# Issuing the first three row loads of the first state tile directly behind the store of those rows

## The chip, the cores and the metric

The kernel runs on one core of one Trainium2 chip. The metric is the device time of one launch in microseconds (us); lower is better. The number compared is the median of several launches.

## The reference

The input x is 4 x 1024 tokens of 128 features. Three blocks change it in turn, each with a residual: a mixture-of-experts layer at half weight, a state-space (Mamba) layer, and the same experts again at half weight.

```
x = x + 0.5 * ffn(layernorm(x))
x = x + mamba(layernorm(x))
x = x + 0.5 * ffn(layernorm(x))

ffn:   cw = softmax(x @ w_router) * softmax(x @ w_gating / 0.1), divided by its sum
       out = sum over 8 experts e of cw[e] * ((silu(x @ w_gate[e]) * (x @ w_up[e])) @ w_down[e])
mamba: xs, z = split(x @ W_in);  xc = silu(causal_conv4(xs) + conv_b)
       dt0, B, C = split(xc @ W_x);  dt = softplus(dt0 @ W_dt + b_dt)
       for each token: h = exp(dt * A) * h + (dt * xc) * B;  y = sum over 16 states of h * C
       out = ((y + xc * D) * silu(z)) @ W_out
```

## The kernel before, in words

**Tiles.** The 4096 tokens are cut into eight tiles of 512 tokens. Each tile goes through the experts twice (kind 0 before the Mamba layer, kind 1 behind it), which makes 16 positions. `ORDER` (line 36) fixes their order: tiles 0 to 3 of kind 0, then kinds 1 and 0 by turns. A position has 32 slots: 8 experts times 4 chunks of 128 hidden features. Slot 50, say, is in position 1. A slot is three passes of TensorE for the gate (`first_g`, line 713), a SiLU on ScalarE (`silu`, line 1024), three passes for the up projection (`first`, line 724), their product on VectorE (`first`, line 851) and a down matmul (`down`, line 734), which follows two slots later. Gates run two slots ahead of the up projections. There are three PSUM banks for gates, so the gate of slot i waits for the SiLU of slot i-3 (line 711), and two for up projections, so the up projection of slot i waits for the product of slot i-2 (line 722). At the end of each expert `acc` (line 841) multiplies the expert's output with its token weights, which `cw_load` (line 658) has broadcast from DRAM, and GpSimd issues a DMA that adds it to `ACC` (line 1127).

**The Mamba layer beside it.** Its work on a tile is woven into the slots. `before(t)` (line 181) makes the projections, the convolution, `b_x` (B, C and the input of dt) and dt. `bc_store` (line 643) writes the 32 rows of B and C of 512 tokens from SBUF to the DRAM tensor `BCD`. `scans(t)` (line 267) then goes through the 16 states. For state m (counted over all tiles) `bc_load` (line 650) broadcasts one row of B and one of C to all 128 partitions, into one of `BR` = 3 buffers of `BCB`; `s_b` (line 932) multiplies B with dt * xc; `s_da` (line 1090) makes the decays of two states on ScalarE; `s_scan` (line 943, twice) is the recurrence; `s_hc` (line 951) multiplies with C; and GpSimd issues two DMAs that add the result to `Y` (line 1139).

**What sets the order.** `timetable()` (line 53) runs once on the host. It plays generators (`before`, `scans`, `prep`, `tail`, `closing`) against estimated clocks and appends their steps to one list, `steps`. Each engine then issues its own steps in the order of that list, and waits in order, on semaphores. SyncE's steps, the loads and stores, cost nothing on these clocks. So a step of SyncE takes the place in SyncE's queue at which its generator emitted it.

**Around the change.** For tile 0 the list holds, with the steps of SyncE in bold: `b_x`, **`bc_store` 0**, product 45, `b_dtl`, down 43, `acc` 10, **`cw_load` 13**, gate 48, the `b_dt` steps, ..., `b_dx`, down 47, `acc` 11, **`cw_load` 14**, gate 52, `b_y`, product 50, down 48, gate 53, **`bc_load` 0, 1, 2**, `s_b` 0, `s_b` 1, product 51, `s_da` 0, down 49, the first scan of state 0, gate 54, product 52, down 50, gate 55, product 53, down 51, `acc` 12, **`cw_load` 15**, gate 56, product 54, the layer norm `ln_sum` 3, the second scan, `s_hc` 0, **`bc_load` 3**, and so on. `cw_load` g waits for the `acc` three before it (line 657), so `cw_load` 13 waits for `acc` 10 and `cw_load` 14 for `acc` 11. `bc_load` 0 waits for the landing of `bc_store` 0 (line 647); the loads 0 to 2 wait for nothing else.

The loads are emitted by this helper (line 261), which in the kernel before is called in `scans` alone, at its start and after each `s_hc`:

```
def bc_loads(upto):
    while loaded[0] < upto and loaded[0] // NS in stored:
        step("bc_load", loaded[0])
        loaded[0] += 1
```

Of the kernel before, what the change touches and what calls it, by code (L numbers as in the profile page):

```python
# [31 lines left out]
BR = 3  # L32
# [20 lines left out]
def timetable():  # L53
# [8 lines left out]
    def step(*what, after=0.0, **work):  # L62

        steps.append(what)
        for e, c in work.items():
            clock[e] = max(clock[e], after) + c
            after = clock[e] + SIGNAL[e]
        return after

    def give(b, sem, value, at):  # L70
        free.append((at, b, (sem, value)))
        free.sort(key=lambda f: f[0])

    def until(at):
        while clock["pe"] < at:
            yield False

    def until_v(at):
        while max(clock["v"], clock["pe"]) < at:
            yield False  # L80

    def take():
        while not free or free[0][0] > clock["pe"]:
            yield False
        return free.pop(0)[1:]
# [7 lines left out]
    def rows_of_x():  # L93

        while xn["lock"] or clock["pe"] < xn["at"]:
            yield False
        xn["lock"] = True

    def norm(b, what):
        while ln["lock"]:  # L100
            yield False
        ln["lock"] = True
        q = norms[0]
        norms[0] += 1
        yield from rows_of_x()
        yield from calm()
        at = step("ln_sum", q, b, xn["by"], what, after=clock["pe"], a=1.6)
        yield True
        yield from calm()
        at = step("ln_square", q, b, after=at, a=1.6, p=2.0)  # L110
        yield from until(at + .3)
        at = step("ln_x", q, b, after=at, a=1.5)
        ln["lock"] = False
        yield from until(at + 0.7)
        bk = yield from take()
        at = step("ln_t", q, bk, pe=.6)
        xn.update(by=("m_tr", q + 1), lock=False)
        return q, bk[0], at
# [62 lines left out]
    def before(t):  # L181

        haste.add("before")
        q, b, at = yield from norm(t % XR, ("x1", t))
        haste.clear()
        at = step("b_xn", t, q, b, after=at, a=.52)
        yield from until_v(at + LATEST)
        at = step("b_xl", t, q, b, after=at, v=.75)
        give(b, "v_rm", t + 1, at)
        yield from until(at)  # L190
        for j in range(2):
            bk = yield from take()
            win_at = step("b_in", t, j, bk, pe=.69, a=1.04)
            give(bk[0], "a_win", 4 * t + j + 1, win_at)
            yield True
        yield from until_v(win_at)
        step("b_halo", t, v=.2)
        for q in range(3):
            for j in range(2):
                at = step("b_conv", t, q, j, v=.67)  # L200
                if q != 1:
                    yield True
            if q < 2:
                bk = yield from take()
                give(bk[0], "a_win", 4 * t + q + 3, step("b_in", t, q + 2, bk, pe=.69, a=.52))
                yield True
        yield from until(at - .5)
        for j in range(2):
            at = step("b_silu", t, j, after=at, a=.62)
        yield True  # L210
        yield from until(at)
        yield from rows_of_x()
        bk = yield from take()
        at = step("b_x", t, bk, xn["by"], pe=1.75, a=.9)
        step("bc_store", t)
        xn.update(by=("c_bcd", 16 * (t + 1)), lock=False, at=at + 2.0)
        stored.add(t)
        yield from until_v(at + LATEST)
        at = step("b_dtl", t, bk[0], after=at, v=.61)
        give(bk[0], "v_bc", t + 1, at)  # L220
        yield from until(at)
        for j in range(2):
            bk = yield from take()
            at = step("b_dt", t, j, bk, pe=.47, a=1.1)
            give(bk[0], "a_relu", 2 * t + j + 1, at)
            yield True
        yield from calm()
        at = step("b_soft", t, after=at, a=4.5)
        yield True
        yield from until_v(at + LATEST)  # L230
        at = step("b_dx", t, after=at, v=2.4)
        dt_at[t] = at - 1.2
        decays()
        ready[t] = at
        yield from until_v(at)
        yield from calm()
        step("b_y", t, after=at, a=1.1)
        begun_y.add(t)
        yield True
# [7 lines left out]
    def decays(must=False):  # L247

        m = decayed[0]
        if m < NT * NS and m // NS in dt_at and m + BURST <= done[0] + NA and (must or (  # L250
                dt_at[m // NS] < clock["pe"] + .5 and clock["a"] < clock["pe"] + CALM)):
            at = step("s_da", m, after=dt_at[m // NS], a=2.56 + 1.24 * BURST)
            for k in range(BURST):
                decay_at[m + k] = at
            decayed[0] = m + BURST

    def calm():
        while clock["a"] > clock["pe"] + CALM:
            yield False
# [6 lines that stand above are left out]
# [71 lines left out]
    def mamba_streams():  # L337
        t = begun["closing"]
        if "closing" not in streams and t < NT and t in scanned:
            streams["closing"] = closing(t)  # L340
            begun["closing"] += 1
        t = begun["scans"]
        if "scans" not in streams and t < NT and t in ready and ready[t] < clock["pe"]:
            streams["scans"] = scans(t)
            begun["scans"] += 1
        t = begun["before"]
        if "before" not in streams and t < NT and t in x1 and t <= begun["scans"] and t - 2 in put:
            streams["before"] = before(t)
            begun["before"] += 1
# [42 lines left out]
    for i in range(total):  # L392
# [30 lines left out]
        if p + 1 < NPOS and r >= (PREP if p != 1 else LATER) and p + 1 not in prepared:  # L423
            kind, t = ORDER[p + 1]
# [742 lines left out]
```

## Time and profile before

| what | value |
|---|---|
| median of 3 runs | 1301.04 us (1297.74 to 1301.64) |
| the profiled execution's own time | 1303.95 us |
| its span, first to last instruction | 1302.2 us |
| granted TensorE clock, mean over the span | 0.991 |
| TensorE busy | 1259.6 us (97%) |
| VectorE busy | 1121.7 us (86%) |
| ScalarE busy | 925.3 us (71%) |
| GpSimd busy | 366.8 us (28%) |
| DMA | 208.55 MB, mean 160 GB/s |

The profile describes one execution. Engines are PE (TensorE matmul), PEld (its weight loads), DVE (VectorE), ACT (ScalarE), POOL (GpSimd) and SP (SyncE); a small q marks an engine's instruction queue. Busy time of PE is modelled, since matmuls are pipelined. Times on timelines are microseconds from the start of the span.

### The profile page before, as it was taken

What the parts mean: (1) busy time and instruction counts of PE and PEld (TensorE: products, weight loads), DVE (VectorE), ACT (ScalarE), POOL (GpSimd) and SP (SyncE); (2) the same over time, 40 slices, a digit from 0 to 9 for tenths busy, and PEclk for the clock granted to TensorE, in tenths of its full rate; (3) what the DMA queues carried; (4) which work ended last, traced back from release to release, by engine and by line L of the source; (5) the groups of instructions that cost most, each with busy time, mean ns of one, the idle gap of its engine ahead of it and who ended that gap; (6) DMA issues with size and microseconds to landing.
All of it is one profiled execution on the core that took longest, in us unless ns stands there. A gap on an engine that the chain in (4) does not pass through costs nothing.

```text
span 1302.2 us, 15232 instructions
## 1 busy us (share of the span) xinstructions
PE 1259.6 (97%) x4608; PEld 841.3 (65%) x4608; DVE 1121.7 (86%) x1468; ACT 925.3 (71%) x1757; POOL 366.8 (28%) x438
## 2 busy tenths in 40 slices
PE   5999799999999999999999999999999999999998
PEld 4666566666666666666666666666666665666665
DVE  3554599999999999999989999999999998998343
ACT  6545688878797878887948878698866887653421
POOL 0100134324232322433323332342323323332000
PEclk9999899999999999999999999999999999999899
DMA  6521488789788988987888978987888786895221
GB/s 204 134 54 33 100 177 197 160 176 196 161 181 184 181 173 188 208 177 169 183 180 188 194 171 178 181 191 170 188 175 186 174 186 149 186 197 119 50 64 41
DMA packets 125809, 208.55 MB, mean 160 GB/s; under 512 B 15008, under 2 KB 27808, under 8 KB 125728
## 3 DMA queue, kind: packets, MB, share of 16 engines
q0 software_dynamic: 52128, 94.92, 40.8%
q1 hardware_dynamic: 73600, 112.68, 32.8%
q8 instruction: 36, 0.59, 0.2%
q14 instruction: 45, 0.37, 0.1%
HBM read 109.77 MB, written 2.88 MB: 87 GB/s over the span
## 4 chain that ended last, share of the span: by engine, by line
PE 65%; DMA 12%; ACT 9%; DVE 8%; issue 5%; POOL 2%; SPq 0%; DVEq 0%; ACTq 0%; POOLq 0%
PE PS L734 23%; PE PS L679 13%; PE PS L681 13%; PE PS L680 13%; DMA Y<-HS 7%; DMA ACC<-YE 3%; DVE HS L943 2%; DVE HB L851 2%; DVE HS L951 2%; ACT DA L1090 1%; ACT HB L1024 1%; DMA BCB<-BCD 1%; ACT L1024 1%; PE PS L755 1%; ACT L1090 1%
## 5 line engine op out<-in xcount | busy, mean ns | idle before, releaser
L734 PE MATMUL PS<-HB,WD 128*128 128x512 f32 x1024 | 525.3, 594 | 0.0
L1024 ACT ACTIVATE HB<-PS 128x512 f32<-128x512 f32 x512 | 293.1, 596 | 279.8 <-PE PS L681 277.4
L851 DVE TENSOR_TENSOR HB<-PS,HB 128x512 f32<-128x512 f32 x512 | 347.2, 679 | 113.9 <-PE PS L681 71.7
L679 PE MATMUL PS<-XH,WG 128*128 128x512 f32 x512 | 386.6, 755 | 6.1 <-DVE XH L906 2.0
L1139 POOL DMA_DIRECT2D Y<-HS x252 | 219.7, 949 | 511.0 <-DVE HS L951 319.5
L734 PEld LDWEIGHTS PS<-HB,WD 128*128 128x128 f32 x1024 | 191.8, 189 | 44.3 <-issue 3.4
L679 PE MATMUL PS<-XH,WU 128*128 128x512 f32 x512 | 209.5, 409 | 10.1 <-DVE HB L851 9.8
L1127 POOL DMA_DIRECT2D ACC<-YE x110 | 104.1, 947 | 369.3 <-DVE YE L841 339.4
L681 PE MATMUL PS<-XH,WG 128*128 128x512 f32 x512 | 203.2, 397 | 0.0
L681 PE MATMUL PS<-XH,WU 128*128 128x512 f32 x512 | 202.0, 395 | 0.0
L680 PE MATMUL PS<-XH,WU 128*128 128x512 f32 x512 | 201.0, 393 | 0.0
L680 PE MATMUL PS<-XH,WG 128*128 128x512 f32 x512 | 200.5, 392 | 0.0
L679 PEld LDWEIGHTS PS<-XH,WG 128*128 128x128 f32 x512 | 97.3, 190 | 120.8 <-issue 67.3
L680 PEld LDWEIGHTS PS<-XH,WG 128*128 128x128 f32 x512 | 97.9, 191 | 110.1 <-issue 108.4
L1090 ACT ACTIVATE DA<-XS,aneg 128x512 f32<-128x512 f32 x256 | 164.4, 713 | 2.6 <-DVE HS L943 1.7
L932 DVE TENSOR_TENSOR HS<-BCB,DX 128x1026 f32<-128x1026 f32 (+1 forms) x128 | 155.7, 1220 | 9.2 <-DMA BCB<-BCD 9.2
L943 DVE TENSOR_TENSOR_SCAN HS<-DA,car,HS 128x512 f32<-128x512 f32 x128 | 161.8, 1274 | 0.0
L951 DVE TENSOR_TENSOR HS<-BCB,HS 128x1024 f32<-128x1024 f32 x128 | 156.0, 1219 | 1.1
L943 DVE TENSOR_TENSOR_SCAN HS<-DA,HS 128x513 f32<-128x513 f32 x128 | 155.0, 1219 | 0.1
L679 PEld LDWEIGHTS PS<-XH,WU 128*128 128x128 f32 x512 | 96.7, 189 | 37.0 <-DVE HB L851 15.9
L1024 ACT ACT_TABLE_LOAD x86 | 110.3, 1283 | 2.8 <-PE PS L681 1.1
L681 PEld LDWEIGHTS PS<-XH,WU 128*128 128x128 f32 x512 | 96.7, 189 | 23.2
(104 smaller groups left out, 1127.3 us busy)
## 6 DMA issues: line engine op xcount, KB each, us to landing
BCB<-BCD SPq DMA_DIRECT2D x128, 512.0 KB, 5.6
Y<-HS POOLq DMA_DIRECT2D x252, 256.0 KB, 6.7
CWB<-CWD SPq DMA_DIRECT2D x128, 256.0 KB, 4.3
ACC<-YE POOLq DMA_DIRECT2D x110, 256.0 KB, 5.3
XT<-in_L_attn_x_dram SPq DMA_DIRECT2D x8, 256.0 KB, 5.9
WD<-in_L_ffn_w_down_dram SPq DMA_DIRECT2D x8, 256.0 KB, 6.1
out_dram<-XT SPq DMA_DIRECT2D x8, 256.0 KB, 3.1
HS<-in_L_ffn_w_gate_dram SPq DMA_DIRECT2D x6, 256.0 KB, 5.0
```

The source lines that it names most:

```text
L679: pe.matmul(o, w[0], m[0], start=first, stop=False)
L680: pe.matmul(o, w[0], m[1], start=False, stop=False)
L681: z = pe.matmul(o, w[1], m[0], start=False, stop=last)
L734: pe.matmul(expert(g), WD[:, e, c, :], HB[:, i % NH, :], start=c == 0, stop=c == FC - 1).then_inc(S["m_dn"], 1)
L851: v.tensor_tensor(H, up(i), H, ALU.mult).then_inc(S["v_h"], 1)
L932: v.tensor_tensor(HS[:, m % HR, :, 0:w], rows.unsqueeze(1).broadcast_to([P, 2, w]), DX[:, t % 2, :, 0:w], ALU.mult).then_inc(S["v_db"], 1)
L943: v.tensor_tensor_scan(H, DA[:, m % NA, j, 0:w], H, car[:, j, n:n + 1] if t % 2 else 0.0, ALU.mult, ALU.add).then_inc(S["v_sc"], 1)
L951: v.tensor_tensor(H, BCB[:, m % BR, 1, :].unsqueeze(1).broadcast_to([P, 2, T]), H, ALU.mult).then_inc(S["v_hc"], 1)
L1024: a.activation(HB[:, i % NH, :], gate(i), ACT.Silu).then_inc(S["a_sil"], 1)
L1090: z = a.activation(DA[:, m % NA, j, 0:T], XS[:, t % 2, j, 3:3 + T], ACT.Exp, scale=aneg[:, j, n:n + 1])
L1127: gp.dma_start(ACC[:, :], YE[:, n % 2, :], accum_op=ALU.add).then_inc(S["c_acc"], 16)
L1139: gp.dma_start(Y[:, t % 2, j, :], HS[:, m % HR, j, 0:T], accum_op=ALU.add).then_inc(S[f"c_y{j}"], 16)
```

## The change

Directly behind the store of tile 0's rows, and for tile 0 only, the helper is called with `BR` = 3, so that `bc_load` 0, 1 and 2 stand right behind `bc_store` 0 in SyncE's queue and ahead of `cw_load` 13 and 14. The call at the start of `scans(0)` then finds nothing left to emit. All other steps keep their order.

```
--- before.py
+++ after.py
@@ -215,6 +215,8 @@
         step("bc_store", t)
         xn.update(by=("c_bcd", 16 * (t + 1)), lock=False, at=at + 2.0)
         stored.add(t)
+        if t == 0:
+            bc_loads(BR)
         yield from until_v(at + LATEST)
         at = step("b_dtl", t, bk[0], after=at, v=.61)
         give(bk[0], "v_bc", t + 1, at)
```

## Rows read from the trace of the kernel before

**Rows 1.** The page: busy time by engine, and the group of line 932.
```profile
PE 1259.6 (97%) x4608; PEld 841.3 (65%) x4608; DVE 1121.7 (86%) x1468; ACT 925.3 (71%) x1757; POOL 366.8 (28%) x438
...
L932 DVE TENSOR_TENSOR HS<-BCB,DX 128x1026 f32<-128x1026 f32 (+1 forms) x128 | 155.7, 1220 | 9.2 <-DMA BCB<-BCD 9.2
```

**Rows 2.** Busy time by stretch of 10 us; last three columns: PE clock, DMA share, GB/s.
```profile
140.00:150.00 10.00, 5.08 (x19) 3.18 (x17) 2.50 (x5) 8.03 (x11) 0.85 (x1) 1.00 0.78 202
150.00:160.00 10.00, 8.18 (x22) 5.41 (x22) 7.28 (x9) 3.38 (x17) 0.85 (x1) 0.66 0.28 59
160.00:170.00 10.00, 10.00 (x37) 6.72 (x36) 9.97 (x12) 9.53 (x18) 6.39 (x8) 1.00 0.70 146
```

**Rows 3.** Waits, 125 to 175 us: total us, times, longest us.
```profile
DVE HS L932 <- DMA BCB<-BCD: 7.5, 2, 6.9
```

**Rows 4.** Timeline of SyncE: start, us, engine, line, operation, count.
```profile
127.13 0.33 SPq L643 DMA_DIRECT2D BCD<-XN  x1
128.83 12.13 SPq L658 DMA_DIRECT2D CWB<-CWD  x2
141.01 1.47 SPq L650 DMA_DIRECT2D BCB<-BCD  x3
```

**Rows 5.** Landings: store, loads at 141.0-142.0, `cw_load` 13, adds at 129.1 and 140.9.
```profile
BCD<-XN SPq DMA_DIRECT2D x1, 64.0 KB, 1.6
...
DMA to landing us min/median/max: 7.1/8.4/9.2
...
CWB<-CWD SPq DMA_DIRECT2D x1, 256.0 KB, 3.4
ACC<-YE POOLq DMA_DIRECT2D x1, 256.0 KB, 4.3
...
ACC<-YE POOLq DMA_DIRECT2D x1, 256.0 KB, 8.0
```

**Rows 6.** Timeline of VectorE; in brackets the idle time before and what ended it.
```profile
140.53 0.68 DVE L851 TENSOR_TENSOR HB<-PS,HB 128x512 f32<-128x512 f32 x1
148.14 1.23 DVE L932 TENSOR_TENSOR HS<-BCB,DX 128x1026 f32<-128x1026 f32 x1 [6.92 <-DMA BCB<-BCD]
149.94 1.23 DVE L932 TENSOR_TENSOR HS<-BCB,DX 128x1026 f32<-128x1026 f32 x1 [0.57 <-DMA BCB<-BCD]
151.09 0.68 DVE L851 TENSOR_TENSOR HB<-PS,HB 128x512 f32<-128x512 f32 x1
...
155.22 0.69 DVE L841 TENSOR_TENSOR YE<-PS,CWB 128x512 f32<-128x512 f32 x1 [0.95 <-PE PS L734]
157.55 0.69 DVE L851 TENSOR_TENSOR HB<-PS,HB 128x512 f32<-128x512 f32 x1 [1.65 <-PE PS L681]
...
167.00 0.68 DVE L841 TENSOR_TENSOR YE<-PS,CWB 128x512 f32<-128x512 f32 x1
```

**Rows 7.** Timeline of TensorE: gates 54 and 55, up 53, gate 61.
```profile
141.59 0.79 PE L679 MATMUL PS<-XH,WG 128*128 128x512 f32 x1
...
143.83 0.79 PE L679 MATMUL PS<-XH,WG 128*128 128x512 f32 x1
...
144.69 0.40 PE L681 MATMUL PS<-XH,WG 128*128 128x512 f32 x1
151.82 0.79 PE L679 MATMUL PS<-XH,WU 128*128 128x512 f32 x1 [6.74 <-DVE HB L851]
...
166.69 0.79 PE L679 MATMUL PS<-XH,WG 128*128 128x512 f32 x1
```

**Rows 8.** Timeline of ScalarE: first decays, SiLUs 54 and 55, 56, 58 and 59.
```profile
143.18 2.56 ACT L1090 ACTIVATE DA<-XS,aneg 128x512 f32<-128x512 f32 x4
...
147.05 1.09 ACT L1024 ACTIVATE HB<-PS 128x512 f32<-128x512 f32 x2
156.56 0.60 ACT L1024 ACTIVATE HB<-PS 128x512 f32<-128x512 f32 x1 [8.42 <-PE PS L681]
...
165.90 1.08 ACT L1024 ACTIVATE HB<-PS 128x512 f32<-128x512 f32 x2
```

More of the change, by code:

```diff
@@ L217, in before @@
         stored.add(t)
+        if t == 0:
+            bc_loads(BR)
         yield from until_v(at + LATEST)
```

## The prediction

> **What bounds the kernel now.** I read the page first: TensorE is busy 97% of the span, and line 932, the first reader of the loads, is idle for 9.2 us in all its 128 instances, always for a landing [rows 1]. Next, the waits between 125 and 175 us: 7.5 of these 9.2 us fall here, in two waits, the longest 6.9 [rows 3]. So the first state tile alone has a hole, and seven later tiles hardly any. The busy time by stretch shows what it does: between 140 and 150 us TensorE falls to 5.08 of 10 us and VectorE to 2.50, and from 150 to 160 the granted clock is 0.66, a mixture of TensorE's two levels, 1.2 and 2.4 GHz; from 160 on TensorE, VectorE and ScalarE are all busy 95% or more [rows 2].
>
> The timelines give the cause, step by step. The store is issued at 127.13 [rows 4] and lands 1.6 us later [rows 5], at 128.7. The three loads need nothing else, yet are issued from 141.01 on, because `cw_load` 14 stands ahead of them in SyncE's queue: the row at 128.83 holds `cw_load` 13 and 14 and lasts 12.13 us, nearly all of it the wait for `acc` 11 [rows 4]. The loads land 7.1, 8.4 and 9.2 us after their issues [rows 5], so VectorE, ready at 141.2, starts `s_b` 0 at 148.14 and, after 0.57 us more, `s_b` 1 at 149.94 [rows 6]. Product 51 is queued behind both and starts at 151.09 [rows 6]. TensorE needs it for up 53, which starts at 151.82 after 6.74 us idle [rows 7].
>
> **What the hole costs.** Gates 54 and 55 start at 141.59 and 143.83, so an unhindered slot is 2.24 us. Gate 61 is six slots on and would start at 143.83 + 13.44 = 157.27; it starts at 166.69 [rows 7]. The loss is **9.42 us**. Some 6.9 of it is the hole: the last gate pass of slot 55 starts at 144.69 and lasts 0.40 us, and since passes overlap its successor would have started within it, at about 144.9, against 151.82. The other 2.5 us is the half clock that TensorE was granted just after it had stood idle [rows 2].
>
> **The change, part by part.**
>
> *The three loads, moved.* They pass `cw_load` 13 and 14. SyncE now waits for the store's landing at 128.7 and issues the loads at about 128.8, 129.3 and 129.8 (1.47 us for three [rows 4]). With the landings of before they are there at 135.9, 137.7 and 139.0. VectorE wants the first at 141.2 and the second at 142.4. That leaves 5.3 and 4.7 us of slack. Even a landing of 9.2 us for each, the longest of the three [rows 5], leaves 3.2 for the first. A store landing of 1.6 us could double and nothing would wait. Cost of the move: nothing, as long as this slack holds; past it, each us late is a us of hole.
>
> *SyncE's new wait.* Behind the waiting `bc_load` 0 stand `cw_load` 13 and 14. The first moves from 128.83 to about 130.3, a 1.5 us delay, and now shares the DMA engines with the 1.5 MB of the loads. No row shows such a load behind three others: 3.4 us is its landing alone, 9.2 that of the slowest load [rows 5], so bounds of 3.4 and about 10. I take the far one, since it queues behind them, so 140.3. Its reader is `acc` 13, which ran at 167.00 [rows 6] and would move to some 157.6: 17 us of cover. `cw_load` 14 still waits for `acc` 11 and keeps its time of 140.6. Cost 0.
>
> *GpSimd's add at 129.1.* It took 4.3 us there, and 8.0 us when issued at 140.9 beside the three loads [rows 5]. The two swap: the add at 129.1 lands near 137, the one at 140.9 near 145.2. The next add isn't issued before 140.9, and `acc` 12, which waits for the buffer of `acc` 10's add, wants it at about 146.9. Cost 0.
>
> *VectorE with the rows there.* `s_b` 0 at 141.2, `s_b` 1 at 142.3, product 51 at 143.5, done by 144.2, before up 53 wants to start at about 144.9. The first scan then meets the decays: four activations take 2.56 us from 143.18 [rows 8], so state 0 has both at 144.46, a new wait of at most 0.4 us. Product 52 follows at 145.7, 53 at 146.3 and `acc` 12 at about 146.9. Product 54 needs SiLU 54 (147.6 [rows 8]) and up 54 (148.0 at 2.24 us a slot), so starts at 148.05 against 157.55 [rows 6]: 9.5 us earlier. TensorE has no hole and so no reason that these rows show for the half clock.
>
> *ScalarE, late next.* It doesn't gain all of that. It was busy until 148.14 and then idle for 8.42 us until SiLU 56 [rows 8]. With gate 56 done by 147.4 it runs on without a stop, but no more than 8.42 us earlier. From there to 167 us its work is packed (9.53 of 10 us [rows 2]). The pair of SiLUs 58 and 59 starts at 165.90 and takes 1.08 [rows 8], so 58 is done at about 166.5, and in the new kernel at 158.1. Gate 61 waits for it and wanted 157.27: it starts at about 158.2. TensorE gives back **0.9 us**, and the shift behind it is 8.5.
>
> *Behind it.* All later work hangs on these engines by waits alone, in an unchanged order. Nothing in the loop runs to a date of its own: the loads of x that come later wait for stores of the output. So a shift common to all engines travels to the end. SyncE's and GpSimd's queues are idle at 157 us, as they would be at 148.
>
> **The sum.** 9.4 - 0.9 = 8.5 us. The profiled execution took 1303.95 us, 1.75 more than its span, and so 2.9 above the median of the runs. On it the new time is 1295.4; on the median, 1301.04 - 8.5 = **1292.5 us**.
>
> *A rule that judges the bound otherwise.* TensorE's busy time here is 10.00 of 10 us and its weight loads 6.72, with VectorE at 9.97 [rows 2]. The Trainium skill, "Perfetto Trace Analysis", section "Identifying the Most-Contended Engine", holds matmul busy time to be a poor measure of TensorE's headroom, and has one look at the weight loads' share and at the occupancy of the other engines. By that rule VectorE paces this stretch, and the sum would go by VectorE's idle time, which is the first rival below.
>
> **The rivals.**
>
> 1. *VectorE paces, and ScalarE's hold doesn't count.* VectorE's idle times in the hole are 6.92, 0.57, 0.95 and 1.65 us, in all 10.1 [rows 6]. Of these the new order keeps none to 0.6 us (the waits for the decays and for up 54), so 9.5 to 10.1 us: 1291.0 to 1291.5. For it: 9.97 of 10 us. Against it: a gate that starts 0.9 us late on a TensorE without any idle time. Chance 0.13.
>
> 2. *A part comes back.* Behind the hole TensorE, VectorE and ScalarE are packed, and some wait that the hole had hidden appears later, or the half clock strikes at another, shorter stop. Losing the clock's 2.5 us again gives 1295.0; losing half of the hole too, 1298. For it: the engines leave the stretch at slightly different shifts. Against: the order and all durations are the same. Chance 0.14.
>
> 3. *Nothing is gained.* The hole is replaced, or the gain is absorbed wholly: the loads land just as late relative to VectorE, because the row data or a wait unseen behind the queue's holds them. Then 1301 (1297.2 to 1304.9). That the loads don't move at all would be the same; but the tile is in `stored` when the helper is called, so they are emitted. Against it: the store's landing at 128.7. Chance 0.07.
>
> 4. *Slower: the loads collide with the add of `acc` 10.* Place: the DMA engines, 129 to 139 us. The add (256 KB, issued by GpSimd) and the loads (1.5 MB) overlap, as the row of 8.0 us shows [rows 5]. `acc` 12 on VectorE waits for that add, and product 54 stands behind it. It decides from an add that lands later than 146.9, 17.8 us after its issue; only beyond 17.8 + 8.5 + 3.9 = 30 us would the kernel be slower by more than can be told. An add of 35 us would give 1306. With 8.0 us measured beside the same three loads, the chance is 0.02. The Trainium skill, "DMA: Bandwidth & Descriptors", section "Issuing engines are not separate DMA queues", says that DMAs of all issuing engines run on the same 16 engines and interleave; by that rule moved loads slow whatever they now meet, and the trace agrees (4.3 against 8.0 us).
>
> **How the numbers follow.** A measurement of this kernel tells about 0.3% from no change, 3.9 us. The forecast, 8.5 us with 7.5 to 9.4 as its own bounds, has 0.64. With the rivals at 0.13, 0.14, 0.07 and 0.02 that makes 1. Cases 1 and the forecast are faster by over 3.9 us; of case 2 some four fifths are. So faster 0.88, same 0.09, slower 0.03 (case 4 and a little noise). The runs of before spread over 3.9 us, so I set the range at 1288.5 (10.1 us gained and 2.4 of that spread) to 1296.5 (4.5 gained, most of case 2).
>
> **What would show it.** Right: three issues of line 650 at 128.8 to 130.3, landed before 140; no wait of line 932 in this stretch; up 53 at about 144.9; a clock of 1.00 from 150 to 160; SiLU 56 at about 148.1 and gate 61 at 158.2; the later waits as before. Wrong: line 932 or the first scan waiting by over 1 us at 141 to 145, `acc` 12 waiting for a DMA, gate 61 at 157.3 (rival 1), or matched steps that stand 8.5 us earlier at 170 us but less at 400 or 1200 us (rival 2).

## The result and the profile after

The changed kernel takes 1293.26 us (median; 1293.18 to 1294.78) against 1301.34 us for the kernel before, run beside it (1297.74 to 1302.05). The ratio is 0.9932, with a 95% interval of 0.9916 to 0.9947: 8.1 us faster, between 6.9 and 10.9. The forecast was 1292.5 us. Its profiled execution took 1293.2 us with a span of 1291.4. Two lines were added above them, so line 932 of before is line 934 now, 650 is 652, and so on.

SyncE's timeline of the changed kernel, to be held against [rows 4]:

```profile
127.15 0.33 SPq L645 DMA_DIRECT2D BCD<-XN  x1
128.85 1.41 SPq L652 DMA_DIRECT2D BCB<-BCD  x3
130.30 17.68 SPq L660 DMA_DIRECT2D CWB<-CWD  x3
```

The store is issued where it was, and the three loads follow at 128.85 instead of 141.01. `cw_load` 13 now comes at 130.30; 14 and 15 share its row and hold nobody up.

VectorE's timeline, against [rows 6]:

```profile
141.14 2.36 DVE L934 TENSOR_TENSOR HS<-BCB,DX 128x1026 f32<-128x1026 f32 x2
143.41 0.69 DVE L853 TENSOR_TENSOR HB<-PS,HB 128x512 f32<-128x512 f32 x1
144.64 1.23 DVE L945 TENSOR_TENSOR_SCAN HS<-DA,HS 128x513 f32<-128x513 f32 x1 [0.54 <-ACT DA L1092]
...
146.96 0.68 DVE L843 TENSOR_TENSOR YE<-PS,CWB 128x512 f32<-128x512 f32 x1
148.13 0.69 DVE L853 TENSOR_TENSOR HB<-PS,HB 128x512 f32<-128x512 f32 x1 [0.49 <-PE PS L683]
```

Both readers of the rows run back to back from 141.14, without a wait. Two small waits are new: 0.54 us for the decays and 0.49 us for up 54. Product 54 starts at 148.13 instead of 157.55, 9.42 us earlier.

TensorE's timeline (up 53, gate 61) and ScalarE's (SiLUs 54 to 56, SiLUs 58 and 59), against [rows 7, 8]:

```profile
144.93 0.39 PE L681 MATMUL PS<-XH,WU 128*128 128x512 f32 x1
...
158.04 0.51 PE L681 MATMUL PS<-XH,WG 128*128 128x512 f32 x1 [0.21 <-ACT HB L1026]
```

```profile
147.07 1.57 ACT L1026 ACTIVATE HB<-PS 128x512 f32<-128x512 f32 x3
...
157.39 1.09 ACT L1026 ACTIVATE HB<-PS 128x512 f32<-128x512 f32 x2
```

Up 53 starts at 144.93, so the hole is gone. SiLU 56 follows 54 and 55 directly, and gate 61 waits for SiLU 58, as forecast.

Busy time by stretch of 10 us, against [rows 2]:

```profile
140.00:150.00 10.00, 10.00 (x38) 6.90 (x37) 8.94 (x13) 9.84 (x21) 1.71 (x2) 1.00 0.36 77
150.00:160.00 10.00, 9.79 (x36) 6.19 (x35) 9.97 (x12) 9.91 (x23) 5.90 (x8) 1.00 0.78 165
```

TensorE's busy time goes from 5.08 and 8.18 us to 10.00 and 9.79, and the granted clock of the second stretch from 0.66 to 1.00.

**Does the shift travel to the end?** One instruction for each position, VectorE's first reduction for the gating, can be followed through both traces (line 799 before, 801 after):

```profile
177.97 0.20 DVE L799 TENSOR_REDUCE mx<-PS 128x8 f32<-128x64 f32 x1
...
634.75 0.22 DVE L799 TENSOR_REDUCE mx<-PS 128x8 f32<-128x64 f32 x1
...
1109.71 0.21 DVE L799 TENSOR_REDUCE mx<-PS 128x8 f32<-128x64 f32 x1
...
1220.65 0.21 DVE L799 TENSOR_REDUCE mx<-PS 128x8 f32<-128x64 f32 x1
```

```profile
168.74 0.20 DVE L801 TENSOR_REDUCE mx<-PS 128x8 f32<-128x64 f32 x1
...
625.30 0.22 DVE L801 TENSOR_REDUCE mx<-PS 128x8 f32<-128x64 f32 x1
...
1100.47 0.22 DVE L801 TENSOR_REDUCE mx<-PS 128x8 f32<-128x64 f32 x1
...
1209.44 0.22 DVE L801 TENSOR_REDUCE mx<-PS 128x8 f32<-128x64 f32 x1
```

The shift is 9.23, 9.45, 9.24 and then 11.21 us. In this pair of executions it arrives whole. The step at the end has nothing to do with the loads: both kernels stop TensorE shortly before that point, in the same place of the program, and in this pair the kernel before was at half clock for longer. Four microseconds of each at about the same distance behind that stop:

```profile
1216.00:1220.00 4.00, 4.00 (x15) 3.52 (x14) 0.00 (x0) 1.88 (x2) 0.00 (x0) 0.50 0.00 0
```

```profile
1206.80:1210.80 4.00, 4.00 (x17) 2.64 (x16) 1.05 (x3) 2.23 (x4) 0.00 (x0) 0.70 0.00 0
```

So the spans differ by 10.8 us, the medians by 8.1, and the early part of the traces by 9.2. The last is the least touched by chance, and the experiments are read by it. Two limits belong to it. The kernel before has a single trace, so how much the half clock behind its hole varies from one execution to the next is not shown. And late steps move by chance in one and the same kernel: a second trace of the changed kernel stood 0.14 us later than the first at the reduction of position 2 and 2.76 us earlier at that of position 14 (1097.71 against 1100.47).

### The profile page after: what moved, and what is told of

Its sections match the earlier page's. It is cut to its first block, busy times and chain, and to the rows that moved or that the text cites. A ratio compares the mean times of both kernels' runs of the same rounds, so it can differ in the third digit from the quotient of the medians.

```text
span 1291.4 us, 15232 instructions
## 1 busy us (share of the span) xinstructions
PE 1256.1 (97%) x4608; PEld 838.3 (65%) x4608; DVE 1121.2 (87%) x1468; ACT 925.1 (72%) x1757; POOL 364.9 (28%) x438
## 4 chain that ended last, share of the span: by engine, by line
PE 66%; DMA 11%; ACT 9%; DVE 8%; issue 5%; POOL 1%; DVEq 0%; SPq 0%; ACTq 0%; POOLq 0%
PE PS L736 23%; PE PS L681 13%; PE PS L683 13%; PE PS L682 13%; DMA Y<-HS 8%; DMA ACC<-YE 2%; DVE HS L945 2%; DVE HS L953 2%; ACT DA L1092 2%; DVE HB L853 2%; ACT HB L1026 1%; ACT L1026 1%; ACT L1092 1%; DVE HS L934 1%; PE PS L757 1%
```

## How the experiments are read

Single executions differ by several microseconds, with the mean granted clock: runs of the kernel before went from 1296.57 us at 0.995 to 1307.54 us at 0.989. The early part of the traces agrees far more closely: eight traces in which the loads come in time, and no step of an engine is moved before the second mark, have between 68.75 and 68.80 us between the two marks below. I use two marks: VectorE's addition at the end of position 0 (99.94 us before) and the reduction of position 2 (177.97). The time between them is 78.03 us in the kernel before and 68.78 in the changed one (168.74 - 99.96), a gain of 9.25. Taking a difference between marks also removes the start, which varies by up to 1.6 us. Where one execution was measured, its total time alone says little: six executions of the changed kernel on one chip went from 1290.43 to 1297.77 us.

## Was it the place in SyncE's queue?

```
--- before.py, at the end of timetable()
+    steps.remove(("cw_load", 14))
+    steps.insert(steps.index(("bc_load", 2)) + 1, ("cw_load", 14))
```

> The kernel before, with one step moved: cw_load 14 stands behind bc_load 0 to 2 in SyncE's queue instead of ahead of them; the loads are still emitted by scans(0). If the only thing that held the loads was the in-order wait of cw_load 14 for acc 11, they are issued at about 129.2 us (behind cw_load 13), land before 140, line 932 does not wait, and the time is that of the changed kernel, 1292 to 1294.5. If the gain needed the place directly behind the store, or came from something else that moved, the time stays above 1297.

Measured: 1293.98 us (ratio 0.994, 0.9925 to 0.9955), and 68.75 us between the marks, a gain of 9.28. The loads were issued from 129.89, right behind `cw_load` 13 at 129.51.

```profile
129.51 0.33 SPq L660 DMA_DIRECT2D CWB<-CWD  x1
129.89 1.46 SPq L652 DMA_DIRECT2D BCB<-BCD  x3
141.29 7.34 SPq L660 DMA_DIRECT2D CWB<-CWD  x2
```

The time and the issues met the expectation. The whole gain comes from getting the loads out from behind one DMA that waited for `acc` 11. Being directly behind the store has no worth of its own.

## How late may the loads be?

Four kernels delay the loads by making `bc_load` 0 wait for one more event, or by moving fewer of them. The diffs, all against the changed kernel:

```
 wt.wait_ge(S["c_bcd"], 16 * (t + 1))
+if m == 0:
+    wt.wait_ge(S["a_relu"], 2)      # at_relu
+    wt.wait_ge(S["a_soft"], 1)      # at_soft
+    wt.wait_ge(S["v_dt"], 1)        # at_dt
```

(one of the three waits in each kernel), and

```
-            bc_loads(BR)
+            bc_loads(1)             # one_early
```

> The changed kernel, with bc_load 0 also waiting for the last Relu of dt in tile 0, so that the loads are issued at about 132.3 us: 3.4 us later than in the changed kernel and 4 us earlier than in at_soft. This measures the slack, put at 5.3 us for the first load and 4.7 for the second. Theory: with landings of 5.4 and 7.4 us, as in the changed kernel, the rows are there at 137.7 and 140.2; nothing waits, and steps at 178 us stand 9.2 to 9.3 us earlier than in the kernel before (8.6 from a common start), the same as in the changed kernel. If the second load lands as late as in at_soft (9.5 us), it comes at 142.3, just in time, with a wait of 0.3 us at most. A wait of 1 us or more would say that the slack was put too high.

> The changed kernel, with bc_load 0 also waiting for the softplus of tile 0 on ScalarE, so that the loads are issued at about 136.3 us instead of 128.9. Theory (the cost is what the landing is late against VectorE at 141.2, and the half clock comes only behind a long stop): with landings of 5.4 to 7.1 us the first row is there at 141.7 to 143.4, up 53 is 0 to 2 us late, the granted clock stays at 1.00, and the time is 0 to 2 us above the changed kernel. Rival (any stop of TensorE here also costs half clock): 2 to 4.5 us above it.

> The changed kernel, with bc_load 0 also waiting for VectorE's first operation of b_dx in tile 0, so that the loads are issued at about 138.9 us, 2.1 us ahead of the kernel before. Theory: a stop of TensorE of 3 to 4.5 us; if the half clock follows it the loss against the changed kernel is 5.5 to 7 us (1298.5 to 1300.5), if it does not the loss is only the stop, 3 to 4.5 us (1296 to 1298). A loss of 9 us, as in the kernel before, would say that the date of the issue isn't what sets the hole.

> The changed kernel with one load early; loads 1 and 2 stay behind cw_load 14 and are issued at about 141 us. Theory: the first reader doesn't wait, the second waits for a landing at 146.5 to 149, TensorE stops for 3.5 to 5.5 us. At_soft stopped it for 3.07 us and kept the full clock, at_dt for 5.14 us and lost it, so either can follow; steps behind 170 us stand 3 to 6 us later than in the changed kernel. Rival (the first row alone sets the hole): no stop.

("8.6 from a common start" in the first was a slip; from the common mark the changed kernel gains 9.25.)

| kernel | loads issued, on the changed kernel's scale | TensorE stops before up 53 | between the marks | gain | time |
|---|---|---|---|---|---|
| changed | 128.85 | no | 68.78 | 9.25 | 1293.26 |
| at_relu | 132.34 | no | 68.76 | 9.27 | 1295.49 (one run) |
| at_soft | 136.30 | 3.07 us | 71.92 | 6.11 | 1297.4 (0.9953 to 0.9979) |
| one_early | 129.01, two at 141.04 | 3.48 us | 72.38 | 5.65 | 1297.69 (one run) |
| at_dt | 138.82 | 5.14 us | 76.19 | 1.84 | 1299.29 (0.9967 to 0.9997) |
| before | 141.03 | 6.74 us | 78.03 | 0 | 1301.34 |

(The issues are those of the traces less the difference of the first marks, 0.77 us for at_relu, 0.15, 0.24 and 0.85 for the next three.)

VectorE of at_relu, VectorE of at_soft, and TensorE of at_soft, one_early and at_dt:

```profile
141.89 2.36 DVE L936 TENSOR_TENSOR HS<-BCB,DX 128x1026 f32<-128x1026 f32 x2
```

```profile
141.69 1.23 DVE L936 TENSOR_TENSOR HS<-BCB,DX 128x1026 f32<-128x1026 f32 x1 [0.33 <-DMA BCB<-BCD]
146.42 1.23 DVE L936 TENSOR_TENSOR HS<-BCB,DX 128x1026 f32<-128x1026 f32 x1 [3.50 <-DMA BCB<-BCD]
```

```profile
148.30 0.50 PE L683 MATMUL PS<-XH,WU 128*128 128x512 f32 x1 [3.07 <-DVE HB L855]
```

```profile
148.84 0.50 PE L681 MATMUL PS<-XH,WU 128*128 128x512 f32 x1 [3.48 <-DVE HB L853]
```

```profile
151.08 0.79 PE L683 MATMUL PS<-XH,WU 128*128 128x512 f32 x1 [5.14 <-DVE HB L855]
```

At_relu met its expectation: a delay of 3.5 us costs nothing. Its second load was issued at 133.54 us of its own trace and took 8.7 us, so it landed 0.8 us before VectorE wanted it at 143.0. At_soft met its expectation in kind (full clock, a short stop) but not in size. I had allowed 0 to 2 us and it was 3.1, which is the rival's size; it is the clock of 1.00 that speaks against the rival. The first load landed 5.2 us after its issue, but the second 9.5 us after, where 7.4 was its landing in the changed kernel. Why is open. `cw_load` 14 and the add of `acc` 11, both issued at about 141, met its transfer; but in at_relu these came only 0.6 us before the second load landed, and it took 8.7 us all the same. So it is the second load that sets this hole, and its slack is smaller than a constant landing time says. At_dt fell outside its expectation: the stop was 5.14 us where 3 to 4.5 were forecast, and the loss 7.4 where 5.5 to 7 were, because its second load too took 9.1 us. One_early lost 3.6 us, within its 3 to 6, with a stop of 3.48 us at the edge of the 3.5 to 5.5 forecast; its rival, that the first row alone sets the hole, fell.

The half clock separates the table in two. In at_soft and one_early the loss against the changed kernel is 3.14 and 3.60 us, which is the stop (3.07 and 3.48) and nothing else. In at_dt the loss is 7.41 for a stop of 5.14, and in the kernel before 9.25 for 6.74: 2.3 and 2.5 us more (one trace of each kernel). Stretches of 5 us show why, first one_early, then at_dt:

```profile
150.00:155.00 5.00, 5.00 (x19) 3.20 (x17) 4.50 (x6) 3.47 (x18) 0.85 (x1) 1.00 0.39 91
```

```profile
150.00:155.00 5.00, 3.92 (x7) 2.49 (x8) 3.96 (x6) 0.00 (x0) 0.00 (x0) 0.50 0.27 76
```

One_early kept 2.4 GHz; at_dt was granted 1.2 GHz and did 7 matmuls in the 3.9 us behind its stop, where the other did 19 in 5. The sizes fit too. In steps of 1 us the granted clock of at_dt is 0.50 up to 155 and 0.63 from 155 to 156, that of the kernel before 0.50 up to 156 and 0.52 from 156 to 157, so TensorE worked at half clock for about 4.7 us behind the stop in the one and 5.1 in the other (estimates from these clocks). Half of that is 2.3 and 2.6 us. The split of the forecast, a hole of 6.9 us and 2.5 us for the clock, is borne out by this.

```
-            bc_loads(BR)
+            bc_loads(2)             # two_early
```

> The changed kernel with two loads early instead of three; load 2 is issued where it was before, behind cw_load 14, at about 141 us. Its reader is s_b 2 at 151.1 us, so it has 10 us and lands in 5 to 7. Theory: no wait, the time of the changed kernel within 1 us, and cw_load 13 and the add at 129.1 land earlier than with three (10.8 and 10.5 us there, 7 to 9 here). Rival (all three loads were needed): 2 us or more slower.

Measured: 68.76 us between the marks, a gain of 9.27, and 1291.6 us (0.9899 to 0.9943). The third load may stay where it was. The median is 1.7 us below that of the changed kernel, but the intervals overlap and the early part of the traces shows no cause. What differs lies late: the profiled execution of two_early kept the full clock behind the stops near 1075 and 1203 us, where that of the changed kernel fell to half. A part of the expectation missed: with two loads the add at 129 still took 10.8 us to land and `cw_load` 13 10.4, no better than with three. In two_and_decay, which also has two loads early, they took 9.3 and 8.8.

## Could the moved loads do harm?

```
 (behind bc_load 2, on SyncE)
+for k, D in enumerate((DX[:, 1, :, 0:T], SZ[:, 1, :, :], Y[:, 1, :, :])):
+    sy.dma_start(D, BCD[0, :, k:k + 1, :]...broadcast_to([P, 2, T])).then_inc(S["c_dum"], 16)
 (ahead of cw_load 15)
+wt.wait_ge(S["c_dum"], 48)
```

> The changed kernel with three more broadcasts of rows of BCD (0.5 MB each, into buffers of tile 1 that nothing reads before they are rewritten) right behind bc_load 2: 3 MB instead of 1.5 at 129 us. This tests the slower rival. If a late add of acc 10 (10.5 us with 1.5 MB) is what threatens, it now lands 14 to 20 us after its issue, near the 17.8 us from which acc 12 waits: a wait of acc 12 of 0 to 3 us. If the add keeps a fair share beside the queue of loads, it lands within 12 us and nothing waits. Rows 0 and 1 should still be there at 141.2 in either case, since their loads stand first.

Measured: 1293.25 us in one run, 68.77 us between the marks, a gain of 9.26. With 3 MB queued by SyncE the add landed after 8.7 us; in the changed kernel, with 1.5 MB, it took 10.5. The transfers at 130 us, the two later loads and the add:

```profile
BCB<-BCD SPq DMA_DIRECT2D x2, 512.0 KB, 7.0
ACC<-YE POOLq DMA_DIRECT2D x1, 256.0 KB, 8.7
```

In this execution the add issued by GpSimd did not queue behind SyncE's loads: it landed before the last of them, and doubling what SyncE had queued did not slow it. The slower rival would have needed 30 us.

## Does ScalarE hold the gain back?

```
--- the changed kernel, at the end of timetable()
+    steps.remove(("s_da", 2))
+    steps.insert(steps.index(("silu", 58)) + 1, ("s_da", 2))
```

> The changed kernel with the decays of states 2 and 3 (step s_da 2, with its two table loads) moved behind SiLU 58 in the list. This tests the hold by ScalarE. Theory: SiLU 58 is done by 153, gate 61 starts at 157.5 instead of 158.04 without a wait, and TensorE stands 0.4 to 0.6 us earlier at 158; the decays still are there before the scan of state 2 at 159.9. Whether that half a us is left behind 180 us is open: by theory yes where TensorE paces, no where VectorE does.

Measured: 1290.61 us in one run. Gate 61 starts without a wait:

```profile
158.82 0.79 PE L683 MATMUL PS<-XH,WG 128*128 128x512 f32 x1
```

This execution's first mark stands at 101.50, 1.54 us later than in the changed kernel, so on that scale gate 61 is at 157.28 instead of 158.04. The first pass of a gate is shorter after a wait (0.51 against 0.79 us), so the hold cost TensorE 0.5 us, not the 0.8 between the starts: in the changed kernel gate 62 starts at 160.01, 1.97 us after gate 61 and not 2.24. At the second mark 0.19 us of it is left (68.59 against 68.78; two_and_decay, which moves the same step, has 68.60). The hold is real and worth next to nothing.

## Which engine paces the scans?

Both kernels are the changed one with work added in positions 3 to 12, and compute the same.

```
# pe_extra, in the up projection of every fourth slot
+                if twice:
+                    pe.matmul(o, w[0], m[0], start=True, stop=True)
# dve_extra, before every second acc
+                    if 3 <= p < 13 and g % 2 == 0:
+                        wt.wait_ge(S["dv"], dv)
+                        own(v.tensor_tensor(JUNK[:, :], expert(g), CWB[:, g % CR, :], ALU.mult))
```

> The changed kernel with 80 more TensorE passes, one in every fourth up projection of positions 3 to 12 (the first pass is issued twice; the first issue is overwritten), 0.23 us each, 18.4 us in all. If TensorE paces the stretch in which the scans run, the time grows by 15 to 19 us. If VectorE paces it (rival 1), by under 6.

> The changed kernel with 40 more products on VectorE, one before every second acc of positions 3 to 12, of the same operands into a buffer that nothing reads, 0.60 us each from start to start, 24 us in all. If VectorE paces the stretch of the scans (rival 1), the time grows by 20 to 24 us; if TensorE does, by under 6; a share for each says that they pace by turns.

Measured: 1304.13 and 1310.66 us in one run each, with spans of 1302.3 and 1308.9 us against 1291.4, at the same mean clock of 0.996. The 18.4 us of TensorE passes cost 10.9 us and the 24 us of VectorE products 17.5: 59% and 73%. A single execution can be off by some microseconds, so the traces were compared as well. From the reduction of position 2 to that of position 14, twelve traces in which nothing is added to these positions (that of the kernel before among them) need 928.4 to 931.7 us, pe_extra 940.8 and dve_extra 947.5. That makes 9 to 12.5 us for the passes (49% to 68%) and 16 to 19 for the products (66% to 80%). Both expectations for a single pacing engine fell. The reading that fits is that the two pace by turns, with half or more of the work added to either paid; where each does is not shown. For this change that made no difference, since the hole stopped both.

## The two together

> The changed kernel again, as a yardstick on the same chip for two_and_decay: 1292 to 1295 us, ratio 0.992 to 0.9955.

> Two loads early (as in two_early) and the decays of states 2 and 3 behind SiLU 58 (as in decay_later). By theory two loads early cost and gain nothing against three, and the decays gain at most 0.5 us, so the time is that of the changed kernel within 1.5 us; a real gain of the two-load version (its median lay 1.7 us below) would show as 1.5 us or more.

The changed kernel again: 1293.99 us, ratio 0.9951 (0.9932 to 0.997). Two early loads with the decays moved: 1292.31 us, ratio 0.9938 (0.9922 to 0.9954). The intervals overlap widely; there is no version here that is shown to beat the changed kernel.

## Why the prediction was right, point by point

**The cause of the hole** was `cw_load` 14's wait for `acc` 11 in SyncE's queue, as forecast. Shown by cw_behind: moving that one step gives the whole gain.

**The loss of 9.42 us**, read as six slots that took too long, was right: up 53 and product 54 came 6.9 and 9.4 us earlier, and 9.25 us were left at the second mark. Its split into hole and half clock agrees with at_soft, one_early and at_dt.

**The cost of 0 for the moved step** held, with the sizes off both ways. The landings were 5.4, 7.4 and 10.6 us instead of 7.1, 8.4 and 9.2. `cw_load` 13 took 10.8 us to land, so was there at 141.1, near the 140.3 that I had taken from the far bound, with 16 us to spare. The add took 10.5 us and not 8.0; 17.8 was its limit. One figure of the rival on the add was worked out wrongly: an add of 35 us would have held `acc` 12 for 35 - 17.8 = 17.2 us, and 1301.04 - 8.5 + 17.2 is 1309.7 us, not 1306.

**The slack** was put at 5.3 and 4.7 us. A delay of 3.5 us cost nothing and one of 7.4 us cost 3.1. A slack of 4.3 for the second load agrees with both, and with the 0.8 us that at_relu had left. The forecast gave the second load the smaller slack; it is the one that sets the hole, and 4.7 was close.

**ScalarE's hold** was over-sized: 0.9 us of the sum, 0.5 measured at gate 62 and 0.2 at the second mark. This is the term that put the shift at 8.5 where the traces show 9.2. The step that failed is "TensorE gives back 0.9 us": it took the delay of the gate's start for the loss, though the first pass behind the wait was shorter (0.51 us against 0.79).

**Rival 1** said that VectorE paces and 9.5 to 10.1 us come. The traces show 9.25, between it and the forecast, and gate 61, which it wanted at 157.3, started at 158.04 behind a wait for ScalarE. By the Trainium skill, "Perfetto Trace Analysis", section "Identifying the Most-Contended Engine", matmul busy time says little of TensorE's headroom. The added work bears it out in part: work added to VectorE, busy for 87% of the span, was paid to a larger share than work added to TensorE at 97%. But TensorE's weight loads, 65% busy, would have one expect more room than half or more of the added passes being paid. **Rivals 2, 3 and 4** didn't come: the shift between 178 and 1110 us of the kernel before stays within 8.8 and 9.9 us in the pair of traces above, and the add had 7 us left.

**The median** came out 8.1 us lower, near the forecast's 8.5, but that is partly the luck of a few executions: the same two kernels gave ratios of 0.9932 and 0.9951, 8.1 and 7.6 us between the medians with the second interval from 3.9 to 8.9, on two occasions.

## What to carry to other kernels

SyncE issued its DMAs in the order of its queue in every trace here, so a load that is ready can stand behind one that is waiting for an engine, here for 12 us; when a reader idles for a landing, look at what stands ahead of the issue in its queue before blaming the transfer. The order of steps that cost nothing on a planner's clocks still has to be planned. And read the price of a hole from the same step some slots later, since the half clock behind it belongs to it.

## What was unexpected of the hardware

The loss jumped with the length of the stop in this place: stops of 3.07 and 3.48 us cost 3.1 and 3.6, one of 5.14 us cost 7.4, because in these traces the granted clock stayed at 1.00 with the first two and went to 1.2 GHz with the last, as it had behind the 6.74 us of the kernel before.

The length of one stop doesn't decide it alone, though. In the changed kernel TensorE stops for 2.58 us at 1073 us, and from 1076 to 1080 the granted clock is 0.67; in a second execution of it, the same stop of 2.58 us left the clock at 1.00. The stop near the end, at about 1203 us, was followed by half clock of different lengths in the kernel before and the changed one, worth 2 us, and by none in two_early. So the same stop can cost something or nothing, and stops of 3.07 and 3.48 us, seen in one execution each, are no proof that stops of that length are free. These chances explain much of the spread of the runs: between mean clocks of 0.989 and 0.995 lie 0.006 x 1300 = 7.8 us of TensorE's time (an estimate from these clocks), of the 11 us between those two runs.

How fast a transfer landed depended on what else was in flight, in no simple order. The add at 129 us took 3.3 to 4.3 us in four traces with no row load beside it, 7.4 beside one, 9.3 and 10.8 beside two, 10.4 to 10.7 beside three in five traces, but 7.6 beside three that stood behind `cw_load` 13 (cw_behind), and 8.7 beside six. I have no explanation for the last two, and no run separates the causes.
